# Even slots of a fused attention and FFN kernel: third query projection ahead of the values, both halves of V directly behind them, last query projection behind V

## What is computed

```python
q = (layernorm(x) @ Wq)   # 32 heads of 128
k = (ctx @ Wk)            # 8 key heads of 128
v = (ctx @ Wv)
q = q * cos + rotate_half(q) * sin
k = k * cos + rotate_half(k) * sin
attn = softmax(where(mask, q @ k.T / sqrt(128), -1e9))
x = x + (attn @ v) @ Wo
# the FFN: a router of 8 experts scales a sign-weight product
r = softmax(layernorm(x) @ gate_w.T)
x = x + (layernorm(x) * (r @ in_scale)) @ sign(weight).T * (r @ out_scale) + bias
```

## Time and profile before

| quantity | value |
|---|---|
| median of 3 runs | 1145.2 us (1145.05 to 1145.42) |
| the profiled execution's own time | 1146.23 us |
| its span | 1144.3 us |
| TensorE busy | 1132.6 us, 99% |
| VectorE, GpSimd, ScalarE busy | 813.3, 704.8, 537.0 us |
| DMA engines, mean | 92 GB/s, q1 28.4% of 16 engines' span |

### The profile page before, as it was taken

The page is one execution under the profiler, slowest core; times in us unless marked ns, Lnnn a source line. Parts: engine busy times, 40 slices in busy tenths (PEclk is TensorE's granted clock), DMA queues, the critical chain, the costliest instruction groups (busy, mean ns, idle before and its releaser), DMA issues.

```text
span 1144.3 us, 22925 instructions
## 1 busy us (share of the span) xinstructions
PE 1132.6 (99%) x7935; PEld 955.1 (83%) x7935; DVE 813.3 (71%) x1366; ACT 537.0 (47%) x1736; POOL 704.8 (62%) x585
## 2 busy tenths in 40 slices
PE   9999999999999999999999999999999999999998
PEld 8778888888888888888888888888888888888877
DVE  5876876767687766877767676677767767776577
ACT  4554454454544454444553535544444544445443
POOL 5855675555667556675665666566675556755544
PEclk9999999999999999999999999999999999999999
DMA  8323332333323223333422323333232222322301
GB/s 243 103 85 101 115 122 79 90 97 92 91 82 102 75 82 84 123 107 93 116 81 73 103 74 86 98 99 114 84 89 78 75 83 75 86 80 74 93 20 38
DMA packets 134483, 105.29 MB, mean 92 GB/s; under 512 B 10680, under 2 KB 109256, under 8 KB 134400
## 3 DMA queue, kind: packets, MB, share of 16 engines
q1 hardware_dynamic: 128848, 93.72, 28.4%
q10 hardware_dynamic: 4784, 8.40, 2.2%
q0 software_dynamic: 768, 2.10, 0.6%
HBM read 100.00 MB, written 4.19 MB: 91 GB/s over the span
## 4 chain that ended last, share of the span: by engine, by line
PE 93%; DVE 3%; issue 2%; ACT 1%; POOL 1%; DMA 1%; ACTq 0%; DVEq 0%; POOLq 0%
PE chunk L1256 22%; PE chunk L1258 21%; PE chunk L1257 21%; PE duo_ps L1332 6%; PE duo_ps L1245 3%; PE o_ps L1355 3%; PE aux L1245 2%; PE duo_ps L1355 2%; PE chunk L1308 1%; PE chunk L1310 1%; PE chunk L1309 1%; DVE swp L943 1%; PE o_ps L1310 1%; PE o_ps L1309 1%; PE o_ps L1308 1%
## 5 line engine op out<-in xcount | busy, mean ns | idle before, releaser
L455 POOL TENSOR_TENSOR w_lo<-raw,w_hi 128x512 fp32r<-128x512 f32 x192 | 247.7, 1303 | 314.7 <-ACT w_hi L598 312.3
L943 DVE TENSOR_TENSOR swp<-chunk,sinT 64x512 f32<-64x512 f32 x320 | 220.3, 688 | 51.2 <-PE chunk L1258 32.1
L598 ACT ACTIVATE w_hi<-raw 128x512 fp32r<-128x512 f32 x192 | 116.6, 630 | 274.3 <-PE chunk L1258 208.8
L1256 PE MATMUL chunk<-xT_hi,w_hi 128*128 128x512 f32 x512 | 206.7, 404 | 1.5 <-POOL w_lo L455 1.5
L1258 PE MATMUL chunk<-xT_hi,w_lo 128*128 128x512 f32 x512 | 200.3, 391 | 0.0
L1257 PE MATMUL chunk<-xT_lo,w_hi 128*128 128x512 f32 x512 | 199.7, 390 | 0.0
L1256 PE MATMUL chunk<-wo_hi,oT_hi 128*128 128x512 f32 x492 | 195.1, 396 | 1.2 <-DVE oT_lo L877 1.2
L1258 PE MATMUL chunk<-wo_hi,oT_lo 128*128 128x512 f32 x492 | 191.9, 390 | 0.0
L1257 PE MATMUL chunk<-wo_lo,oT_hi 128*128 128x512 f32 x492 | 191.7, 390 | 0.0
L635 ACT ACTIVATE probs<-scores,neg_max 128x64 f32<-128x64 f32 x512 | 170.4, 337 | 41.1 <-DVE neg_max L899 41.1
L462 POOL TENSOR_TENSOR qT<-qT,swp 128x512 f32<-128x512 f32 x127 | 163.8, 1297 | 34.6 <-DVE qT L945 34.0
(11 more groups left out here) (284 smaller groups left out, 2046.5 us busy)
## 6 DMA issues: line engine op xcount, KB each, us to landing
raw<-in_L_xattn_Wq SPq DMA_DIRECT2D x128, 256.0 KB, 2.8
raw<-in_L_xattn_Wo SPq DMA_DIRECT2D x128, 256.0 KB, 2.7
raw<-in_L_xattn_Wk SPq DMA_DIRECT2D x32, 256.0 KB, 2.8
raw<-in_L_xattn_Wv SPq DMA_DIRECT2D x32, 256.0 KB, 3.0
acc<-in_x ACTq DMA_DIRECT2D x14, 256.0 KB, 2.7
x_tile<-in_x SPq DMA_DIRECT2D x12, 256.0 KB, 2.9
c_tile<-in_ctx SPq DMA_DIRECT2D x12, 256.0 KB, 3.2
result<-y ACTq DMA_DIRECT2D x12, 256.0 KB, 2.0
```

The source lines that it names most:

```text
L455: nc.gpsimd.tensor_tensor(lo, raw[:, r, :], hi.bitcast(F32), ALU.subtract).then_inc(wsplit_lo, 1)
L598: return nc.scalar.activation(dst, src, ACT.Copy)
L943: last = nc.vector.tensor_tensor(swp[to, k, :], bank[of, :], sinT[to, here], ALU.mult)
L1256: nc.tensor.matmul(bank, a_hi, b_hi, start=opens and i == 0, stop=False)
```

## The change

In even slots the order on TensorE becomes: query 2, query 3, values, (router transpose), V half 0, (in scales), V half 1, (out scales), query 4, (FFN product). The weight stream of even slots becomes K, query 1, 2, 3, Wo 0, V of the next head, V of its own, query 4, Wo 1, 2, 3. V half 0 goes to `chunk[2]` and half 1 to `chunk[0]`. VectorE makes both low parts of V in the even slot itself, behind the low parts of the outputs and ahead of the last rotation, where they stood at the head of the odd slot. ScalarE copies V's half 0 behind weight tile 7, then half 1, and only then the high parts of tiles 8, 9 and 10, the last three Wo tiles. GpSimd's order is as it was.

```diff
--- before.py
+++ after.py
@@ -52,9 +52,10 @@
 
 
     V_OWN, V_NEXT = PROJ - 1, CH
-    EVEN_STREAM = [0, 1, 2, 3, 6, 4, V_OWN, V_NEXT, 7, 8, 9]
+    EVEN_STREAM = [0, 1, 2, 3, 6, V_NEXT, V_OWN, 4, 7, 8, 9]
     ODD_STREAM = [0, 1, 2, 3, 6, 7, 4, 8, 9]
     FIRST_STREAM = [0, V_NEXT, V_OWN, 1, 2, 3, 4]
+    EVEN_RANK = {0: 0, 1: 1, 2: 2, 3: 3, V_NEXT: 4, V_OWN: 5, 4: 6}
     assert CH == 2 * RING and PROJ % WRING == 0 and BT == 512 and 2 * S == P and KVH == TJ + PAIRS + 2
 
     x_t = x.rearrange("(n b) s e -> n (b s) e", b=2)
@@ -135,7 +136,7 @@
         sc_ps, tr_ps = (duo_both[:, i, :] for i in range(2))
 
         DUO_BANK, TABLE_BANK = [sc_ps, tr_ps], o_ps[1]
-        V_BANK, FIRST_V_BANK = [chunk[1], o_ps[0]], [chunk[0], sc_ps]
+        V_BANK, FIRST_V_BANK = [chunk[2], chunk[0]], [chunk[0], sc_ps]
         OUTPUTS = [o_both, duo_both]
         C_BANK, X_BANK = [aux, sc_ps, tr_ps, o_ps[0]], [sc_ps, tr_ps, aux, chunk[2]]
         X_ORDER = [0, 2, 1, 3]
@@ -290,7 +291,7 @@
 
         def rank(s, c):
 
-            return FIRST_STREAM.index(c) if s.first_proj else PROJ if c == V_NEXT else c
+            return FIRST_STREAM.index(c) if s.first_proj else c if s.odd else EVEN_RANK[c]
 
         def entry(s, c):
 
@@ -622,7 +623,7 @@
                 if i == 0:
                     act.wait_ge(v_half, s.U + 2)
                 else:
-                    act.wait_ge(proj_done, proj_count(s, V_OWN if s.first_proj else V_NEXT))
+                    act.wait_ge(proj_done, proj_count(s, V_OWN))
                 copy(two_tiles(v_hi, i), v_bank(s, i)[:, :]).then_inc(v_h, 1)
 
             def exp_duo(s, d, part=range(8)):
@@ -787,17 +788,17 @@
                     split_hi(s, 8)
                 else:
                     split_hi(s, 7)
+                    v_hi_split(s, 0)
                 if s.ffn:
                     xs_split(f[0], in_slot)
+                if not s.odd:
+                    v_hi_split(s, 1)
+                if s.ffn:
+                    out_scales(f[0], in_slot)
                 if not s.odd:
                     split_hi(s, 8)
                     split_hi(s, 9)
                     split_hi(s, 10)
-                if s.ffn:
-                    out_scales(f[0], in_slot)
-                if not s.odd:
-                    v_hi_split(s, 0)
-                    v_hi_split(s, 1)
                 if s.ffn:
                     store(f[0], in_slot)
                 if s.residual:
@@ -1059,10 +1060,6 @@
                     for j in range(1, KQ):
                         rotate(s, j)
                     return scales_lo()
-                if s.odd:
-                    even = Slot(s.q, s.g - 1, False, False, odd=0)
-                    v_lo_split(even, 0)
-                    v_lo_split(even, 1)
                 if s.intake:
                     pick_positions(t[0])
                     x_stats(t[0])
@@ -1110,21 +1107,23 @@
                     rotate(s, 4)
                 else:
                     rotate(s, 1)
-                    if s.ffn:
-                        route_lo(f[0], in_slot)
                     if s.intake:
                         x_lo_split(*t)
                     rotate(s, 2)
+                    rotate(s, 3)
+                    if s.ffn:
+                        route_lo(f[0], in_slot)
                     out_lo(s, 0)
-                    if s.ffn:
-                        scale_in(f[0], in_slot)
-                    rotate(s, 3)
                     out_lo(s, 1)
                 out_lo(s, 2)
                 out_lo(s, 3)
                 if s.number == SLOTS - 1:
                     last_rope_sum(s, KQ - 1)
                 if not s.odd:
+                    v_lo_split(s, 0)
+                    if s.ffn:
+                        scale_in(f[0], in_slot)
+                    v_lo_split(s, 1)
                     rotate(s, 4)
                 if s.ffn:
                     finish(f[0], in_slot)
@@ -1271,10 +1270,10 @@
                     pe.wait_ge(added, n - 2)
                 elif s.after_last:
                     pe.wait_ge(added, (s.U - 3) * PAIRS + p + 1)
+                elif p == 0 and s.odd:
+                    pe.wait_ge(v_ok, s.U + 1)
                 elif p == 0:
                     pe.wait_ge(cos_done, (s.U - 1) * KQ + 3)
-                elif p == 1 and s.odd:
-                    pe.wait_ge(v_ok, s.U)
                 elif p == 1:
                     pe.wait_ge(cos_done, (s.U - 1) * KQ + 4)
                 else:
@@ -1294,13 +1293,12 @@
                 if i == 0:
                     pe.wait_ge(wsplit_lo, split_count(s, max(loads_of(s).index(c) for c in (V_OWN, V_NEXT))))
                     if not s.first_proj:
-                        pe.wait_ge(cos_done, s.U * KQ + 4)
+                        pe.wait_ge(cos_done, s.U * KQ + 2)
                 elif s.first_proj:
                     pe.wait_ge(x_lo, 1)
                 else:
-                    pe.wait_ge(o_lo, (s.U - 1) * PAIRS + 2)
-                lowest = min(entry(s, V_OWN), entry(s, V_NEXT))
-                both = slice(lowest, WRING, 1 if s.first_proj else 2)
+                    pe.wait_ge(cos_done, s.U * KQ + 3)
+                both = slice(entry(s, V_NEXT), entry(s, V_OWN) + 1)
                 for t in range(2):
                     here = span(s.side * BT + (2 * i + t) * P, P)
                     bank = v_bank(s, i)[:, bass.ts(t, 2 * D)].rearrange("p (g d) -> p g d", g=2)
@@ -1373,6 +1371,8 @@
                     pe.wait_ge(cos_done, s.U * KQ)
                 elif j == 2:
                     pe.wait_ge(cos_done, (s.U - 1) * KQ + 3)
+                elif j == 4 and not s.odd:
+                    pe.wait_ge(v_ok, s.U + 1)
                 else:
                     pe.wait_ge(cos_done, s.U * KQ + j - 2)
                 n = entry(s, j)
@@ -1504,24 +1504,27 @@
                 if s.ffn:
                     t_logits(f, in_slot)
                 project(s, 1 if s.odd else 2)
+                if not s.odd:
+                    project(s, 3)
                 values(s, 0)
                 values(s, 1)
                 if s.ffn:
                     t_route(f, in_slot)
-                project(s, 2 if s.odd else 3)
-                if s.ffn:
-                    t_in_scales(f, in_slot)
-                project(s, 3 if s.odd else 4)
-                if s.ffn:
-                    t_out_scales(f, in_slot)
                 if s.odd:
-                    project(s, 4)
+                    project(s, 2)
                 else:
                     v_rows(s, 0)
                 if s.ffn:
+                    t_in_scales(f, in_slot)
+                if s.odd:
+                    project(s, 3)
+                else:
+                    v_rows(s, 1)
+                if s.ffn:
+                    t_out_scales(f, in_slot)
+                project(s, 4)
+                if s.ffn:
                     t_product(f, in_slot)
-                if not s.odd:
-                    v_rows(s, 1)
 
             def product_hi(f, b):
                 pe.wait_ge(osc_ok, f + 1)
```

## The result

The changed kernel takes 1207.26 us, the median of 4 runs (1206.34 to 1208.11), against 1145.17 us (1145.05 to 1145.42) for the kernel before: a ratio of 1.0541, with a 95% interval of 1.0528 to 1.0554. That is 62.1 us more where 46.0 were forecast; it lies inside the range.

A forecast was written before the change was run, and what follows sets the result against it. TensorE, busy 99% of the span, was taken to bound the kernel. Stands of 34.7 us (9 slots) and 11.3 us (6 slots, removed wait deducted) sum to 46.0 us, giving 1191.2 us; range 1186 to 1211.

The forecast's parts named there:

- What bounds the kernel: TensorE is busy 99% of the span, so nearly every microsecond added or left open there is time.
- the first rival: TensorE's clock falls in the gaps: 2.15 us more per stand, 1210 us for 9 long stands, 1223 with all; chance 0.17.
- What the change takes away: V half 0's wait for VectorE in even slots with an FFN tile: 0.34 us in each of 6, 2.0 us.
- the joints: Places on TensorE where reordered work meets: taken as 0, bounded by 0.1 us a slot either way.
- What it adds: Late Wo copies make a 6.61 us chain after V half 1; TensorE stands 3.86 us in 9 slots, 2.23 in 6.
- a sign: First output product waits for GpSimd's `wo_lo` 15 times, 9 of about 3.8 us, 6 of about 2.2, 45 to 50 in sum.
- The start after a wait: TensorE's second matmul after a wait follows after 0.22 us, usually 0.12: 0.10 us more, counted in the chain.
- What is late next: Work behind the stand, such as rope 4 for the scores (8.97 us against 9.45), stays hidden; nothing further waits.
- The norm on VectorE: Next tile's norm in 6 slots with an FFN tile: short value taken, 4.9 us against 5.0, nothing waits.
- the long value: Norm of 1.49 us, not 0.545, only with a GpSimd instruction under way: 0.9 us in each of 6 slots, 5.6 us.
- the 9 long ones: Stands in slots without FFN tile, 3.86 us each; a clock fall in these alone costs 19 us, giving 1210.
- The other rivals: Norm or scores come last, 1197 or 1198 us, chance 0.10; moved copies cost nothing, 1143 us, chance 0.03.

The follow-up runs named there:

- the bank alone: Kernel before with only V half 0 moved to query 2's bank and the odd slot's first output product waiting for its low part: 1143.22 us, ratio 0.9981.
- the first experiment: Changed kernel with ScalarE's high parts of the last three Wo tiles ahead of both V copies: 1161.64 us, ratio 1.0142.
- the filled stands: Changed kernel with 12 unread products (8 in slots with an FFN tile) ahead of the odd slot's first output product: 1192.06 us, ratio 1.0408.

## Why the prediction was right, and where it was not

**What bounds the kernel** was right: 99% TensorE and no wait in the slots meant that each stand would show in full, and it did, in all kernels above. The measured time lies 16 us above the sum of the forecast, and inside the range only because the range took in the first rival.

**What the change takes away**: 0.34 us in each of 6 slots, 2.0 us. Confirmed apart from the rest, 2.2 us by the bank alone. That the joints cost nothing was right within what two kernels can tell (2.4 against 2.2 us).

**What it adds**: the chain was put at 6.61 us from the end of V half 1. It was 535.42 - 528.95 = 6.47 us; GpSimd's four steps took 4.97 us for 5.04, and ScalarE 0.69 for 0.70. The stands were put at 3.86 and 2.23 us and measured 3.75 and 2.17: 46.8 us for 48.1 before the removed wait. In the list of waits they sum to 44.1 us, a little under the 45 to 50 named as a sign, since its idle times are shorter than the stands. The change's part on ScalarE makes them by itself, and undoing it takes them away.

**The start after a wait**, 0.10 us, was the row's value, and right: 535.42 to 535.73 is 0.31 us where 0.23 is usual, 0.08 more. The weight loads of query 4's last product (at 531.47) and of the first output product (at 535.42):

```profile
531.25 0.19 PEld L1257 LDWEIGHTS chunk<-xT_hi,w_lo 128*128 128x128 f32 x1
535.39 0.19 PEld L1255 LDWEIGHTS chunk<-wo_hi,oT_hi 128*128 128x128 f32 x1 [3.95 <-issue]
```

The second begins 0.03 us ahead of its product where the first had 0.22. The Trainium skill, in "TensorE: Matmul & The Clock Gate", section "Step-by-step: what each phase is for", says that TensorE pulls weight loads ahead of matmuls in flight. In this stand none was in flight, and the load was not made ahead.

**What is late next** was wrong in one step and right in another. The step "rope 4 ends 8.97 us after V half 1, and the scores want them at 9.45: hidden" holds only as long as the output product is late itself. I took the stand as given and looked for what lies over the rest, and so did not see that query 4 in the last place leaves 3.7 us of rotation and rope under 2.8 us of work. No time of the changed kernel shows it. It cost 9 x 1.0 us as soon as the first stand was gone, and GpSimd's FFN step, which the prediction does not name and which ends ahead of the late Wo tiles, cost 6 x 1.5. That is why the first experiment missed by 17 us.

**The norm on VectorE** was right: behind the six even slots with an FFN tile it takes 545 to 548 ns each time, where five of the same six took 1.49 us before. All twelve:

```profile
L992 DVE TENSOR_SCALAR x_tile<-acc,f_mv,f_rstd x12: 545/547/1494, 350.8 to 1052.4; 128x512 f32 x12
```

No transpose waited for it. The 24 norms of the two profiled executions tell when it is long: all 11 of 1.49 us began 0.06 to 0.07 us behind an instruction of GpSimd, and none of the 13 of 0.55 us began while GpSimd had one under way. One of each, before and after:

```profile
440.88 2.71 POOL L455 TENSOR_TENSOR w_lo<-raw,w_hi 128x512 fp32r<-128x512 f32 x2
440.95 1.49 DVE L991 TENSOR_SCALAR x_tile<-acc,f_mv,f_rstd 128x512 f32 x1 [0.66 <-POOL f_rstd L476]
```

```profile
465.93 0.55 DVE L992 TENSOR_SCALAR x_tile<-acc,f_mv,f_rstd 128x512 f32 x1 [2.87 <-POOL f_rstd L477]
```

"SBUF — State Buffer" of the Trainium skill, section "SBUF: two separate sides", says that of a VectorE instruction in a two-port mode and one of GpSimd the first to start holds the shared port pair for its whole length. The 24 norms agree with this, though no run took GpSimd's work away alone. The price of the long value was worked out wrongly: 4.3 + 1.49 - 5.0 is 0.8 us a slot and 5 us in all, not 0.9 and 5.6.

**The clock** is where the forecast failed by size: it was the first rival, with 0.17, and it came in the form of "the 9 long ones". The term was 19 us and 15 to 17 were measured (15.2 by the filled stands, 17 by the ten blocks); per stand 1.7 us for 2.15. What misled me was that the trace of before has gaps up to 1.6 us with no fall, from which I argued against it at 3.9 us. The table above has no fall up to 1.55 us either, and 9 of 9 at 3.75: the longest gap of a trace says nothing of one twice as long. "TensorE: Matmul & The Clock Gate" of the Trainium skill, in "Part 1: The HAM clock gate", holds that an idle TensorE goes back to the lower clock. The trace agrees, for 10 of the 15 stands.

**The other rivals** were not seen: neither the norm nor the scores came last in the changed kernel, and the copies were not free.

## What to carry to other kernels

Where one engine is full and another's list has been reordered, count from the last event that the moved entries now stand behind through every queue to the full engine, and compare that chain with the work that lies over it: here 6.5 us over 2.7. Then do it once more as if that stand were gone, since one stand hides the next: here the first one came from three misplaced copies, but the 1.0 and 1.5 us behind it belong to the new order itself. A full TensorE that is made to stand can pay a second time through its clock: here that was a quarter of the loss, and stands of up to 1.55 us never paid it.

## What was not expected of the hardware

The clock fell after stands far shorter than I had thought, and not in a fixed way: in 2 of 9 at 1.9 us and 8 of 9 at 2.6. Products that nobody reads, 2.7 us of them put into each stand of 3.75 and 1.9 us into each of 2.17, saved 15 us of 1207. After a stand of 6.4 us the first product already ran slowly; after one of 3.75 the lower clock came up to 1.1 us behind the start of the first product, in the row shown at the fourth. A fall costs nothing where the work behind it would have had to wait anyway: six of nine in the kernel with GpSimd's Wo tiles first.
